# A pipelined loop of 64 iterations, written out in full, becomes a loop in the program with a body of 4

## The reference

```python
mixed_qkvz = jnp.einsum('bsd,od->bso', x, W_qkvz)
...
qkv = jax.nn.silu(causal_conv4(qkv))              # 4 taps, depthwise
q, k = repeat(rmsnorm(q)), repeat(rmsnorm(k))
M = jnp.where(stril, (k_beta @ k.T) * decay, 0.0)
T = solve_triangular(eye + M, eye)                # per chunk
v_c, k_cumdecay = T @ v_beta, T @ (k_beta * exp(g))
def step(state, inp):                             # over the chunks
    v_new = v_i - k_cumdecay_i @ state
    out_i = (q_i * exp(g_i)) @ state + attn_i @ v_new
    state = state * exp(g_last) + (k_i * exp(g_last - g_i)).T @ v_new
...
out = jnp.einsum('bsf,df->bsd', norm_w * rms(h) * silu(z), W_out)
```

## Time and profile before

| | |
|---|---|
| median of 3 runs | 3829.39 us (3824.57 to 3840.47) |
| the profiled execution | 3829.39 us, its span 3827.5 us |
| TensorE busy | 3328.1 us (87%) |
| VectorE, ScalarE, GpSimd busy | 2712.3, 1887.8, 1255.9 us |
| granted clock, mean | 0.983 of full speed |
| instructions | 57,977 |

### The profile page before, as it was taken

The page is one execution under the profiler, slowest core; times in us unless marked ns, Lnnn a source line. Parts: engine busy times, 40 slices in busy tenths (PEclk is TensorE's granted clock), DMA queues, the critical chain, the costliest instruction groups (busy, mean ns, idle before and its releaser), DMA issues. The chain is left out here.

```text
span 3827.5 us, 57977 instructions
## 1 busy us (share of the span) xinstructions
PE 3328.1 (87%) x18978; PEld 2626.2 (69%) x18978; DVE 2712.3 (71%) x5607; ACT 1887.8 (49%) x4330; POOL 1255.9 (33%) x2441
## 2 busy tenths in 40 slices
PE   0012799999999999999999999999999999999987
PEld 0012677777777777777777777777777777777763
DVE  8995577776777676767777776767677777777743
ACT  4553344555445555544455544555554454555441
POOL 5553333233324233333323332423333333333210
PEclk9999899999999999999999999999999999999998
DMA  2003122222222222222222212222222222222202
GB/s 94 22 32 152 47 70 72 75 64 64 64 75 75 72 75 69 61 67 70 74 74 65 72 53 75 74 73 75 69 57 71 70 75 73 66 72 53 69 5 99
DMA packets 291211, 261.52 MB, mean 68 GB/s; under 512 B 220992, under 2 KB 249792, under 8 KB 281152
## 3 DMA queue, kind: packets, MB, share of 16 engines
q1 hardware_dynamic: 281696, 123.60, 13.5%
q10 hardware_dynamic: 9216, 134.22, 9.5%
HBM read 228.11 MB, written 29.62 MB: 67 GB/s over the span
## 5 line engine op out<-in xcount | busy, mean ns | idle before, releaser
L629 PE MATMUL x<-xs,w_high 128*128 128x512 f32 x3072 | 1066.5, 429 | 39.9 <-POOL w_low L1220 34.5
L629 PE MATMUL x<-xs,w_low 128*128 128x512 f32 x1536 | 613.9, 400 | 0.0
L629 PEld LDWEIGHTS x<-xs,w_high 128*128 128x128 f32 x3072 | 533.6, 194 | 104.4 <-POOL w_low L1220 35.4
L923 ACT ACTIVATE slot<-lane 128x512 fp32r<-128x512 f32 x640 | 351.6, 609 | 482.8 <-PE lane L755 482.7
L864 ACT ACTIVATE uvec<-rb,cpos 128x128 f32<-128x128 f32 x512 | 160.1, 364 | 861.0 <-PE rb L649 861.0
L1203 POOL TENSOR_TENSOR block_step<-block_in 64x14 f32<-64x14 f32 (+6 forms) x896 | 229.1, 256 | 505.4 <-DMA block_in<-blocks_dram 384.7
L1233 POOL TENSOR_TENSOR rstd<-rarg,powers 128x8 f32<-128x8 f32 x64 | 105.0, 1640 | 774.6 <-DVE rarg L1042 774.6
L629 PEld LDWEIGHTS x<-xs,w_low 128*128 128x128 f32 x1536 | 293.3, 191 | 67.8
L755 PEld LDWEIGHTS lane<-pinv,slot 128*128 128x128 f32 x1536 | 202.5, 192 | 181.3 <-DVE pinv L1101 114.7
L755 PE MATMUL lane<-pinv,slot 128*128 128x128 f32 x1536 | 261.7, 309 | 63.9 <-DVE pinv L1101 63.0
L994 DVE SCALAR_TENSOR_TENSOR cacc<-x,cwqk,cacc 128x511 f32<-128x511 f32 (+2 forms) x384 | 281.2, 746 | 44.8 <-ACT cacc L851 22.9
(11 more groups left out here) (202 smaller groups left out, 7480.8 us busy)
## 6 DMA issues: line engine op xcount, KB each, us to landing
xs<-mix_dram ACTq DMA_DIRECT2D x64, 2048.0 KB, 7.6
gb<-cum_dram SPq DMA_DIRECT2D x128, 256.0 KB, 4.5
w_in<-in_w_qkvz SPq DMA_DIRECT2D x48, 512.0 KB, 4.1
w_out<-in_w_out SPq DMA_DIRECT2D x16, 512.0 KB, 4.6
blocks_dram<-bt SPq DMA_DIRECT2D x512, 8.0 KB, 1.5
inverse_dram<-block_out SPq DMA_DIRECT2D x64, 128.0 KB, 2.2
inv<-inverse_dram SPq DMA_DIRECT2D x512, 16.0 KB, 1.9
side_kv<-in_side SPq DMA_DIRECT2D x4, 1024.0 KB, 11.8
```

What stands on the lines that cost most here:

```text
L629: ins = mm(PROJ_BANK[kind][i][:, :], w, x, start=(k == 0 and j == 0), stop=(k == KC - 1 and j == 2))
L923: a(DEST[job][:, h, :, :].rearrange("p c s -> p (c s)"), lane[h][:, :], ACT.Copy).then_inc(copied[h], 1)
```

## The change

`LOOP` calls the body twice with constants, then opens a loop in the program on each engine (`engine.Fori`) that runs 15 times over n = 0, 4, ..., 56, and calls the body four times in it with l, m and n as expressions of the loop's register; then four more calls with constants. Together these are the 66 calls of before. The bodies' conditions on the first and the last iteration can't look at a register's value, so they test whether the argument is a Python integer; the work that they choose is the same in each iteration.

```diff
         def LOOP(engine, body):
 
-            for i in range(ITERS + 2):
-                body(*((i - lag if 0 <= i - lag < ITERS else None) for lag in range(3)), i % BATCH)
+            body(0, None, None, 0)
+            body(1, 0, None, 1)
+            with engine.Fori(0, ITERS - 7, BATCH) as n:
+                for i in range(BATCH):
+                    body(n + (i + 2), n + (i + 1), (n + i) if i else n, (i + 2) % BATCH)
+            body(ITERS - 2, ITERS - 3, ITERS - 4, 2)
+            body(ITERS - 1, ITERS - 2, ITERS - 3, 3)
+            body(None, ITERS - 1, ITERS - 2, 0)
+            body(None, None, ITERS - 1, 1)
...
-                if m > 0:
+                if not (isinstance(m, int) and m == 0):
                     for h in range(HPG):
                         await_product(sp, m - 1, h, 4)
-                if m == 0:
+                if isinstance(m, int) and m == 0:
                     sp.wait_ge(S["zeros_ready"], 1)
...
-                if L and b == 2 and l // BATCH + 1 < HQK:
+                if L and b == 2 and not isinstance(l, int):
                     load_weights(l // BATCH + 1, "qk", l // BATCH + 1)
                 if L:
                     gather_blocks(l, p)
-                    if l < ITERS - 1:
+                    if not (isinstance(l, int) and l == ITERS - 1):
                         load_gates(l + 1, (b + 1) % BATCH, False)
...
-                            if L and l < ITERS - 1:
+                            if L and not (isinstance(l, int) and l == ITERS - 1):
                                 load_input((b + 1) % BATCH)
...
-                if group > 0:
+                if not isinstance(group, int):
                     pool.wait_ge(S[kind + "_full"], group * (2 * BATCH))
...
-                    if b == 3 and l < ITERS - 1:
+                    if b == 3 and not isinstance(l, int):
                         split("qk", (l + 1) // BATCH)
```

More of the change, by code:

```diff
@@ L579, in body @@
                 L, A, B, p = l is not None, m is not None, n is not None, b % 2
-                if l == 0:
+                if L and isinstance(l, int) and l == 0:
                     load_weights(0, "qk", None)
@@ L911, in body @@
                 q = 1 - p
-                if l == 0:
+                if isinstance(l, int) and l == 0:
                     load_input(0)
```

## The result

The changed kernel takes 3950.57 us (median of 4 runs, 3945.06 to 3961.54) against 3831.36 us (4 runs, 3824.57 to 3840.47): 1.0304 times as long, with a 95% interval from 1.0282 to 1.0326. I had forecast 3882 us and a range up to 3945, so the sign was right and the size was not: 53 us were expected, some 119 came. In the profiled execution the span grew by 116 us, from 3827.5 to 3943.2.

A forecast was written before the change was run, and what follows sets the result against it. TensorE, busy 87% of the span, was taken to bound the kernel. Added to 3829.4 us, branches 36, other engines 0, register instructions 6, clock 11 and instruction traffic 0 made 53, so 3882 us; range for 8 in 10 3833 to 3945.

The forecast's parts named there:

- Term 1: Taken branch on TensorE, 14 turns: fetch 3.3 us, 0.7 us covered, 2.6 us each, 36 us (0 to 57).
- Term 2: The same branch on the other engines: fetch 2.5 us each, covered by their waits, nothing on the path.
- rival C: Two fetches per turn on TensorE, or another engine's fetch coming out from under its wait: 3918 us, chance 0.14.
- Term 3: Computed wait values on all engines: 0.1 us exposed in each of 60 iterations, 6 us (0 to 80).
- Rival B: Register instructions not hidden, each computation standing in the chain TensorE, VectorE, ScalarE, TensorE: 3956 us, chance 0.13.
- Term 4: TensorE's clock falling at half the 14 turns, 1.5 us each: 11 us (0 to 21, or below).
- Term 5: Instruction traffic, 3.7 MB of 261 either way: nothing.
- The signs I had named: TensorE hole of 2 to 3 us every fourth iteration, over 152 packets, longer `rb` and `rc` waits only there.
- Rival A: TensorE's turn is free, the target resident or fetched in time: 3835 us, no measurable change, chance 0.16.

The follow-up runs named there:

- experiments 1: Only TensorE runs the program loop, the other four engines written out, against the kernel before: 3945.0 us, ratio 1.0279.
- 6: Only TensorE loops, with a body of 2 iterations instead of 4, the others written out, against the kernel before: 3847.9 us, ratio 1.0038.
- 7: The changed kernel with a body of 12 iterations on all engines, 4 taken branches, against the kernel before: 3874.6 us, ratio 1.0094.
- experiment 12: The changed kernel with SyncE's loads of `gb` and `w_out` at the turn issued later, against the kernel before: 3902.0 us, ratio 1.0180.
- experiment 2: TensorE written out, the other four engines run the program loop, against the kernel before: 3872.7 us, ratio 1.0091.
- experiment 9: The changed kernel with the branch announced on TensorE alone, against the kernel before: 3869.7 us, ratio 1.0080.
- 10: ScalarE, GpSimd and SyncE loop, TensorE and VectorE written out, against the kernel before: 3830.3 us, ratio 0.9990.
- 11: All five loop: TensorE with a body of 2, VectorE and ScalarE with the branch announced, against the kernel before: 3827.2 us, ratio 0.9973.
- experiment 3: The changed kernel with the branch announced at the top of each pass on every engine, against the kernel before: 3845.9 us, ratio 1.0026.
- 5: All written out; at the 14 places TensorE waits for one small SyncE transfer, no branch, against the kernel before: 3921.8 us, ratio 1.0223.
- experiment 8: The changed kernel with 6 unused matmuls queued ahead of TensorE's branch at each turn, against the kernel before: 3932.1 us, ratio 1.0230.

## Why the prediction was wrong

**Term 1, the branch on TensorE: right in kind, short by half in size.** That the body of 2500 instructions isn't kept, that 14 turns miss and that the hole is lost in full was right (experiments 1, 6, 7). The step that failed was "I take the row nearest in kind, a 64 KB load from memory in mid-loop, 2.1 us to landing, plus 1.2 us for a packet": 3.3 us. For a turn at which nothing else moves the total was nearly exact, 3.56 us (experiment 12), but by luck in its parts: the packet starts 1.0 us after the branch and takes 0.9 to 1.3, and the branch ends 1.3 to 1.4 us after the landing, a part that I hadn't thought of. But I took a load's time from a quiet place and moved it to a place where SyncE's `gb` and `w_out`, 1 MB together, are issued. The row was in front of me: the earlier trace rows show `w_out` at 1483.68, 0.1 us after TensorE's sequencer is at the turn. The fetch cost 5.4 us, the holes 69 us and not 36. Even the upper end, 4.8 us and 57 us, was too low, because I built it from single loads too.

**Term 2, the other engines: nil in the sum by luck.** VectorE comes 4.8 to 6.4 us late, not 2.5 (2.7 to 3.0 at a quiet turn); its hole lies beside TensorE's longer one. My remark that with term 1 at nil "the term is still nil but for 0.5 us per turn" was wrong: it is 37 us (experiment 2; 32 in experiment 9, gone in 10). By the record of its packets VectorE fetches twice at a turn, the second packet 2.4 to 2.7 us after the first, so rival C's mechanism was real, on the wrong engine and hidden. ScalarE, GpSimd and SyncE were right.

**Term 3, register instructions:** 6 us expected, nothing found in the changed kernel (51.35 us per iteration) nor in experiments 10 and 11; only experiment 2 has 0.1 us per iteration. Rival B is out, though its 3956 us came nearest to the time: a total near the result is no sign for its mechanism.

**Term 4, the clock:** this is the second step that failed. I priced a fall rightly (1.5 us) and counted wrongly: "I take half the 14 turns". The clock fell at all 14, mostly for 6.8 us and not 3.4, and at 10 turns again some 37 us later, at the place where it also falls in the kernel before. 42 us in the loop, not 11. The length of a fall goes with the hole: behind the 3.3 us of the quiet turn 13 of 14 lasted 3.4 us. The count doesn't: the clock fell at all 14 there, and at all 14 of the short holes, so "half" would have been too few with a fetch of the right size as well. A hole of 2.6 us, as I had it, was not run.

**Term 5:** 37 and 32 more packets, 0.9 MB, nothing, as expected.

**The signs I had named** served: a hole at each fourth iteration released by nothing, more than 152 packets, iterations without a turn unchanged, `rb` and `rc` waited for longer. Rival A needs the fetch to start before the branch; straight code never needs that, and only the announcement (experiment 3) or a body that stays (6) makes the turn cheap. As for the range, its upper end left out the case in which both open prices, fetch and clock, stand above their ends together; they aren't independent, as longer holes bring longer falls.

## What to carry to other kernels

A loop body that doesn't stay on the chip costs a wait for code at each pass. Here 2500 instructions on TensorE, 539 on VectorE and 388 on ScalarE waited, while 1250 on TensorE, 302 on GpSimd and 134 on SyncE didn't; where between them the limits lie wasn't tried. On the engine that bounds, the wait goes on the time. Make the body small enough to stay, or announce the branch, on the bounding engine and on the one next to it. Price such a wait at the place where it falls, with the transfers that are in flight there, and price a hole in TensorE's work as the hole plus the slow matmuls behind it, here 60% on top (34 to 79% in the other rows of the account). When one cost is removed, ask which one lay beside it: VectorE's 37 us were free only as long as TensorE was late.

## What the runs showed of the hardware

- A taken branch on TensorE whose target isn't there: 3.3 to 3.9 us at a quiet turn (experiment 12), 4.6 to 5.8 us with 1 MB of loads in flight (the changed kernel), 5.4 to 7.5 us with the other engines written out (1); with the body kept 0.22 us (6), announced 0.36 us (3), not taken 0.08 us.
- ScalarE's next instruction came 2.4 to 2.7 us after its branch, in bodies of 388 instructions; VectorE's 4.8 to 6.4 us with 539; GpSimd (302) and SyncE (134) had none to wait for.
- Stops of TensorE of 3.3, 3.7 and 5.1 us on the average (experiments 12, 5, the changed kernel) each brought its clock to 1.2 GHz at all 14 places, and useless matmuls in the stop prevented it at 13 of 14 (8).
- The second fall, some 37 us behind the first, isn't a consequence of the first: with the fill (experiment 8) it comes at 13 of the 14 turns, though the first fall is left at one turn alone. It lies where the clock falls in the kernel before as well, 30 to 32 us behind the first `uvec` of an iteration. Why there, and why more often behind a turn, stays open.
